# A graph layer on one core: ScalarE's three DMA issues placed apart, and the z gate placed ahead of the n gate

## What is computed

```python
msg_input = concat([h[src], h[dst]], axis=1)
for t in range(4):
    m = relu(msg_input @ W1[t] + b1[t]) @ W2[t] + b2[t]
    msgs += where(edge_type == t, m, 0)
agg = segment_sum(msgs, dst, num_nodes)
gi = agg @ W_ih.T + b_ih        # parts i_r, i_z, i_n
gh = h @ W_hh.T + b_hh          # parts h_r, h_z, h_n
r = sigmoid(i_r + h_r); z = sigmoid(i_z + h_z)
n = tanh(i_n + r * h_n)
out = x + (1 - z) * n + z * h
```

## Time and profile before

| | |
|---|---|
| median of 3 runs | 1838.65 us (1838.35 to 1839.18) |
| profiled execution, its own time | 1840.2 us |
| its span | 1838.3 us |
| PE busy | 1667.1 us (91% of the span) |
| DVE busy | 1595.2 us (87%) |
| ACT busy | 1494.6 us (81%) |
| POOL busy | 1178.9 us (64%) |
| DMA | 319.72 MB, mean 174 GB/s |
| chain that ended last | PE 73%, ACT 8%, issue 4%, ACT's queue 3%, DVE 2% |

### The profile page before, as it was taken

One profiled execution on the slowest core, in us unless ns is written; L12 is line 12 of the kernel. 1 busy time (PEld: TensorE's weight loads), 2 busy tenths in 40 slices (PEclk: granted clock), 3 DMA queues, 4 the chain that ended last, 5 costly groups with the idle time before them and its releaser, 6 DMA issues.

```text
span 1838.3 us, 43100 instructions
## 1 busy us (share of the span) xinstructions
PE 1667.1 (91%) x10182; PEld 1416.6 (77%) x10182; DVE 1595.2 (87%) x4186; ACT 1494.6 (81%) x3401; POOL 1178.9 (64%) x1982
## 2 busy tenths in 40 slices
PE   0226799999999999999999999999999999999998
PEld 0125688888888888888888888888888888888787
DVE  8597798989888988898889888989899989898776
ACT  0025789889888898898888888889898889888795
POOL 5777777776776777777765656666666566666310
PEclk9999899999999999999999999999999999999999
DMA  2225677777777776777677777777777777777653
GB/s 70 51 48 139 168 195 194 192 192 192 198 187 193 191 194 186 187 192 191 187 193 187 190 188 187 187 190 189 189 190 188 190 186 192 189 187 191 161 136 100
DMA packets 477071, 319.72 MB, mean 174 GB/s; under 512 B 106705, under 2 KB 463009, under 8 KB 476962
## 3 DMA queue, kind: packets, MB, share of 16 engines
q10 hardware_dynamic: 261792, 156.12, 28.6%
q1 hardware_dynamic: 185730, 106.99, 25.3%
q0 software_dynamic: 29440, 55.47, 11.8%
HBM read 211.65 MB, written 106.72 MB: 173 GB/s over the span
## 4 chain that ended last, share of the span: by engine, by line
PE 73%; ACT 8%; issue 4%; ACTq 3%; DVE 2%; DMA 0%; SPq 0%; POOL 0%; DVEq 0%; POOLq 0%
PE bank L1329 16%; PE bank L1331 12%; PE bank L1330 12%; PE bank L1409 10%; PE bank L1399 5%; PE bank L1391 5%; PE bank L1421 3%; PE bank L1420 3%; PE bank L1437 3%; ACT n_h L1194 3%; PE bank L1447 3%; ACT n_zc L1282 2%; ACTq L1211 2%; ACT e_r L1270 2%; ACTq L1232 2%
## 5 line engine op out<-in xcount | busy, mean ns | idle before, releaser
L580 POOL DMA_INDIRECT e_x<-in_x,rows_now x816 | 799.6, 980 | 241.7 <-issue 233.4
L1177 ACT ACTIVATE e_h<-e_x,shift,rstd 128x128 f32<-128x128 f32 x816 | 355.3, 493 | 93.6 <-DVE shift L1048 93.6
L1194 ACT ACTIVATE n_h<-n_x,shift,rstd 128x128 f32<-128x128 f32 x784 | 362.8, 489 | 2.1 <-issue 2.1
L1329 PE MATMUL bank<-n_h_hi,whh_hi 128*128 128x512 f32 x588 | 263.0, 447 | 25.3 <-ACT n_zc L1282 18.3
L1113 DVE TENSOR_TENSOR n_d<-bank,n_n 128x512 f32<-128x512 f32 x196 | 135.5, 691 | 160.7 <-ACT n_n L1278 149.1
L1329 PE MATMUL bank<-n_a_hi,wih_hi 128*128 128x512 f32 x588 | 249.3, 424 | 0.9 <-DVE bank L1083 0.9
L1071 DVE TENSOR_SCALAR n_sel<-iota,n_rel 128x256 fp32r<-128x256 f32 x784 | 237.8, 365 | 8.6 <-POOL n_rel L631 7.2
L1409 PE MATMUL bank<-n_sel,n_win 128*128 128x256 f32 x1568 | 234.9, 292 | 8.6 <-DVE n_sel L1071 8.4
L1331 PE MATMUL bank<-n_h_hi,whh_lo 128*128 128x512 f32 x588 | 232.9, 396 | 0.0
L1330 PE MATMUL bank<-n_h_lo,whh_hi 128*128 128x512 f32 x588 | 232.7, 396 | 0.0
L1331 PE MATMUL bank<-n_a_hi,wih_lo 128*128 128x512 f32 x588 | 232.3, 395 | 0.0
(11 more groups left out here) (179 smaller groups left out, 3895.4 us busy)
## 6 DMA issues: line engine op xcount, KB each, us to landing
n_win<-messages SPq DMA_DIRECT2D x1568, 64.2 KB
messages<-e_msg ACTq DMA_DIRECT2D x204, 257.0 KB, 2.7
n_x<-in_x ACTq DMA_DIRECT2D x195, 256.0 KB
out<-n_out ACTq DMA_DIRECT2D x195, 256.0 KB
e_x<-in_x,rows_now POOLq DMA_INDIRECT x816
rows_now<-lists SPq DMA_DIRECT2D x204, 2.0 KB
lists<-picks,list_rows POOLq DMA_INDIRECT x72
w<-in_W SPq DMA_DIRECT2D x1, 512.0 KB, 4.5
```

The costliest lines, as they stand in the source:

```text
L580: G.indirect_dma_start(e_x[:, s, 2 * end + t, :], None, x, bass.IndirectOffsetOnAxis(ap=rows_now[:, s, t, end:end + 1], axis=0)).then_inc( ...
L1177: last = A.activation(e_h[:, s % 2, k, :], e_x[:, s, k, :], ACT.Relu, scale=rstd[:, slot, col + k:col + k + 1], bias=shift[:, slot, col + ...
L1194: last = A.activation(n_h[:, s % 2, cols], n_x[:, s, cols], ACT.Relu, scale=rstd[:, slot, col + 4 + k:col + 5 + k], bias=shift[:, slot, co ...
L1329: T.matmul(o, w_hi, v_hi, start=start, stop=False, skip_group_check=onto)
```

## The change

ScalarE's step gets another order, and PE's z gate moves ahead of the end of the n gate. The three DMA issues no longer stand in two places but in three: the messages' store after `n_r` with two edge tiles behind it, the output's store after `n_a_hi`, the load of x after `n_zc`. Node tile 0 goes between `n_h_hi` and `n_a_hi`, node tile 1 behind the output's store, node tile 2 behind the load of x and ahead of tanh. `n_zc` goes ahead of tanh, and on PE the z gate goes ahead of the a part of the n gate. `n_h_hi` waits for the count of `n_gate_in` in place of `n_gate_z`, which is now the last of the two to be counted. Nothing that is computed changes.

```diff
--- before.py
+++ after.py
@@ -1233,15 +1233,15 @@
                                   n_out[:, s, :].rearrange("p (k d) -> p k d", k=TILES)).then_inc(n_stored[s], 16)
 
             def step(i, m):
-                normalise_edges(i, m, (0, 1, 2))
+                normalise_edges(i, m, (0, 1))
                 g, s = i - LAG, (m - LAG) % 2
                 if within(g, NG):
                     act.wait_ge(n_gate_r, g + 1)
                     if due(g - 1):
                         act.wait_ge(n_ted, g - 1)
                     A.activation(n_r[:, s, :], bank[BRZ][:], ACT.Sigmoid, bias=bsum[:, 0:1]).then_inc(n_red, 1)
-                normalise_edges(i, m, (3,))
                 store_messages(i, m)
+                normalise_edges(i, m, (2, 3))
                 q, s = i - 8, (m - 8) % 2
                 if within(q, UNITS):
                     act.wait_ge(e_turned, q + 1)
@@ -1252,13 +1252,14 @@
                 if within(g, NG):
                     act.wait_ge(n_turned, g + 1)
                     if due(g - 1):
-                        act.wait_ge(n_gate_z, g - 1)
+                        act.wait_ge(n_gate_in, g - 1)
                     A.activation(n_h_hi[:, s, :], bank[BT[s]][:], ACT.Copy).then_inc(n_hhi, 1)
+                normalise_nodes(i, m, (0,))
+                if within(g, NG):
                     act.wait_ge(n_summed, g + 1)
                     A.activation(n_a_hi[:, s, :], bank[BA][:], ACT.Copy).then_inc(n_ahi, 1)
-                normalise_nodes(i, m, (0,))
                 store_out(i, m)
-                load_x(i, m)
+                normalise_nodes(i, m, (1,))
                 q, s = i - 9, (m - 9) % 2
                 if within(q, UNITS):
                     act.wait_ge(e_hid, q + 1)
@@ -1269,18 +1270,20 @@
                         kind = 2 * ((m - 9) % 2) + t
                         last = A.activation(e_r[:, s, cols], bank[BE1][:, cols], ACT.Relu, bias=b1_cols[:, kind:kind + 1])
                     last.then_inc(e_relued, 1)
-                normalise_nodes(i, m, (1, 2))
                 g, s = i - LAG, (m - LAG) % 2
                 if within(g, NG):
-                    act.wait_ge(n_gate_in, g + 1)
-                    if due(g - 1):
-                        act.wait_ge(n_ded, g - 1)
-                    A.activation(n_n[:, s, :], bank[BIN][:], ACT.Tanh, bias=bih[:, 2:3]).then_inc(n_ned, 1)
                     act.wait_ge(n_gate_z, g + 1)
                     if due(g - 1):
                         act.wait_ge(n_eed, g - 1)
                     A.activation(n_zc[:, s, :], bank[BRZ][:], ACT.Sigmoid, bias=bneg[:, 1:2],
                                  scale=-1.0).then_inc(n_zed, 1)
+                load_x(i, m)
+                normalise_nodes(i, m, (2,))
+                if within(g, NG):
+                    act.wait_ge(n_gate_in, g + 1)
+                    if due(g - 1):
+                        act.wait_ge(n_ded, g - 1)
+                    A.activation(n_n[:, s, :], bank[BIN][:], ACT.Tanh, bias=bih[:, 2:3]).then_inc(n_ned, 1)
                 normalise_nodes(i, m, (3,))
                 q, s = i - 9, (m - 9) % UNROLL
                 if within(q, UNITS):
@@ -1422,10 +1425,10 @@
                     last.then_inc(e_hid, 1)
                 g, s = i - LAG, (m - LAG) % 2
                 if within(g, NG):
+                    pe.wait_ge(n_red, g + 1)
+                    gate(BRZ, 1, s, "ha").then_inc(n_gate_z, 1)
                     pe.wait_ge(n_ted, g + 1)
                     gate(BIN, 2, s, "a", onto=True).then_inc(n_gate_in, 1)
-                    pe.wait_ge(n_red, g + 1)
-                    gate(BRZ, 1, s, "ha").then_inc(n_gate_z, 1)
                 q, s = i - 9, (m - 9) % 2
                 if within(q, UNITS):
                     pe.wait_ge(e_relued, q + 1)
```

More of the change, by code:

```diff
@@ L1271, in step @@
                     last.then_inc(e_relued, 1)
-                normalise_nodes(i, m, (1, 2))
                 g, s = i - LAG, (m - LAG) % 2
+                if within(g, NG):
+                    act.wait_ge(n_gate_z, g + 1)
+                    if due(g - 1):
+                        act.wait_ge(n_eed, g - 1)
+                    A.activation(n_zc[:, s, :], bank[BRZ][:], ACT.Sigmoid, bias=bneg[:, 1:2],
+                                 scale=-1.0).then_inc(n_zed, 1)
+                load_x(i, m)
+                normalise_nodes(i, m, (2,))
                 if within(g, NG):
@@ L1278, in step @@
                     A.activation(n_n[:, s, :], bank[BIN][:], ACT.Tanh, bias=bih[:, 2:3]).then_inc(n_ned, 1)
-                    act.wait_ge(n_gate_z, g + 1)
-                    if due(g - 1):
-                        act.wait_ge(n_eed, g - 1)
-                    A.activation(n_zc[:, s, :], bank[BRZ][:], ACT.Sigmoid, bias=bneg[:, 1:2],
-                                 scale=-1.0).then_inc(n_zed, 1)
                 normalise_nodes(i, m, (3,))
```

## The result

The changed kernel takes **1962.11 us** (median of 4, 1961.9 to 1963.66) against 1838.5 us for the kernel before on the same chips: a ratio of 1.0674, 95% interval 1.0656 to 1.0693. It is slower by 124 us. The forecast was 1975 us, range 1915 to 2010.

The account below looks back on a forecast made before the run. It took an 8.35 us step, with ACT's chain through zc holding PE's r gate, as the bound; the change makes a 9.06 ring (6.21 + 2.85), 192 steps adding 136 to 1840.2, 1976, median 1975 us, range 1915 to 2010.

Parts of the forecast that it names:

- The bound: Whole loop: time is steps times step length, 8.35 us, with a wait for zc and a second nearly tight ring.
- HN's 47.8 us: PE: HN's weight load came just behind DVE's `n_out` 175 times, 47.8 us in all.
- PE's own work: PE per step, without the wait for zc and the 0.18 before the r gate: about 8.06 to 8.10 us.
- the 0.18 ahead of the first r gate: PE, before the r gate of the step examined: 0.18 us counted as removable from the 8.35 step.
- the faster case: If HN did not hang on tanh: step 8.06 to 8.10, 52 us less, 1787 us; chance 5%.
- The z gate first: PE: z done at HN + 5.12, n gate at 5.82; this alone puts tanh at least 0.39 later.
- Zc, load and tile 2 ahead of tanh: ACT: zc at HN + 5.12, plus 0.70 to tile 2 and 0.39 for it, puts tanh at HN + 6.21.
- The ring: HN to HN through zc, tanh and `n_out`: 6.21 + 2.85 = 9.06 us, 192 steps, 136 us more.
- The issues apart: ACT's separated DMA issues: the pause before `e_r` (74.0 us) goes, but slack makes the gain 0.
- The shorter ring: Between zc and tanh, hidden x-load issue or cheaper tile 2: 1900 to 1950 us; chance 16%.
- Long issues: ACT's x load between zc and tanh: one issue in three 0.9 longer, 58 us more, 2033; chance 8%.
- The clock: PE idling about 1 us a step: a tenth of its work at half clock, some 2130 us; chance 4%.

Follow-up runs that it names:

- the same edit alone: Changed kernel with PE's and ScalarE's old gate order and the x load behind tanh, other issue and tile moves kept: 1810.33 us, ratio 0.9846 against the kernel before.
- the gates' part alone: Kernel before with only z gate first on PE and zc right ahead of tanh on ACT, issues and tiles unmoved: 1960.62 us, ratio 1.0668.

## Why the prediction was right, point by point

**The bound.** Right in the main. The kernel's time is the number of steps times a ring, and two rings stood close together. The run that moved `n_e` in the kernel before shows that they even shared a few hundredths, 15 us in all; I had given HN's 47.8 us no part in the bound. PE's own work was read wrongly too: the 0.18 ahead of the first r gate lies before the step of 8.35 and can't be taken from it. Taking off the 0.21 alone gives 8.14. The runs show 8.02 where zc still holds the r gate and 7.92 where nothing does. Only the price of the faster case hung on this, not the forecast.

**The z gate first** (part 1): zc can start at HN + 5.12, and it starts at 1110.93 - 1105.81 = 5.12.

**Zc, load and tile 2 ahead of tanh** (part 2): the one term of the sum that was mis-sized by more than 0.02. I took 0.70 from zc to tile 2, between 0.57 hidden and more; it is 0.60, for the issue begins 0.14 behind zc and not 0.25. With 0.40 for tile 2, tanh is at HN + 6.12 and not 6.21. The end that I had as the lower bound was the better value, and the run with the load behind tanh shows 5 us for the issue.

**The ring** (part 3): 2.85 from tanh to HN, measured 2.83. 9.06 in the forecast, 8.955 measured. 192 steps of 0.71 made 136 us; 195 of 0.607 are 118, so the steps were put 18 us too high. The stretches ahead of the first zc and behind the last, which the forecast left as they were, grew by 1.2 and 2.2 us. The rest of the way to the 13 us by which 1975 was too high is rounding and which run is compared. PE's wait before HN was said to be about 1.0 a step and is 0.79, tanh was said to come 1.1 behind zc and comes 1.00 behind it, DVE's wait for tanh was to grow towards 280 and is 264.7.

**The issues apart** (part 4): right that they bring nothing in the changed kernel, though the reason is in part another: what they win ahead of zc, the load and tile 2 behind it lose. ACT's stand before the messages' store, put at about a microsecond, is 192.3 us over 197 times. The runs add what the page of before could not show: the same edit alone is worth 27 us.

**The rivals.** The faster case fell: PE's wait for `n_out` was no coincidence. Its rule, to find the gaps on the engine one optimizes and make what they wait for start sooner (the Trainium skill, Perfetto Trace Analysis, Optimization Strategy), found a true gap, and the gap closed; but the trace of the changed kernel shows PE waiting 153.1 us for `n_out` where 18.3 us for zc went. The shorter ring is what the runs with tanh behind zc (8.686) and with the load behind tanh (8.931) make of it, but not this kernel. Long issues did not come. They even went: the load of x, issued behind another issue in the kernel before, took up to 1.65 there and at most 0.46 in the changed kernel (its line in both, shortest, median, longest in ns):

```profile
L1211 ACTq DMA_DIRECT2D n_x<-in_x x195: 386/402/1650, 137.0 to 1752.3; - x195
```

```profile
L1211 ACTq DMA_DIRECT2D n_x<-in_x x195: 385/402/459, 138.5 to 1867.5; - x195
```

The clock stayed at 1.00 from 600 to 1600 us though PE stood about 0.8 us in every step. (The Trainium skill, TensorE: Matmul & The Clock Gate, A second HAM failure mode, tells of a kernel whose clock oscillated because of frequent micro-idles between groups of matmuls; this trace has an idle in every step without a change of clock.) The row from 170 to 182 us, which I had taken as the ground for it, was a poor one: right behind it, from 182 to 194 us, the kernel before had PE busy 4.55 of 12 us at a granted clock of 0.50, and from 170 to 182 us the changed kernel had 0.72 with PE busy 8.62.

## What to carry to other kernels

Before swapping two operations on a hand-ordered engine, follow each around the ring that it lies on: from a consumer, through every in-order queue, to the same consumer one step later, and add up the starts; a wait that disappears is worth only the distance to the next ring. An operation whose result nobody needs soon, ahead of one that an engine waits for, is the cheapest thing to move: here one DVE operation moved by three places decided 150 us. Two edits with opposite signs hide each other, so measure them apart; a gain can also be real and show only when another ring has been cut.

## What the runs showed that I had not expected

- An issue of a DMA directly behind an activation cost 0.03 of ACT's time (zc to tile 2 0.60 against 0.57), where two issues in a row cost 0.34; put behind tanh instead, it gave 5 us over the whole kernel. In the three kernels that issue the load of x right behind the output's store (the kernel before, the one with `n_e` moved, the gates' part alone) 13 to 38 of its 195 issues took over 0.6; in the eleven others at most one did.
- Between 110 and 160 us, in the preparation, the granted clock was 0.59 in the changed kernel and 1.00 in the one before, with PE busy about half of the stretch in both. The first zc starts at 205.4 against 204.2 us, so this is worth a microsecond or so. From 120 to 170 us it is the lower of the two levels, 0.50 (1.2 GHz), and PE had done nothing from 120 to 130 us, in the kernel before as well, whose clock stayed at 1.00. It doesn't seem to be the change: the whole-run clock of four runs of the changed kernel is 0.980, 0.981, 0.982 and 0.994, and the last of them is the slowest (1963.66 us); on one of the experiments' chips four of seven runs of the kernel before had 0.98 as well. Why it fell is open.
- Once PE's long waits for zc and `n_out` were gone, POOL's `n_rel` in one step of four was the next to bind in the first half, 1.34 us each time; moving it ahead of two gathers gave 33 us (ratio 0.965 for 0.985).
